# Causal mask of an attention stage: zeros written into the probabilities by GpSimd in place of mask products on TensorE, with the value products two tiles behind

## What is computed

```python
qkv = (x @ Wqkv_w + Wqkv_b).reshape(Bb, Ll, 3, Hh, dd)
scores = jnp.einsum('bhid,bhjd->bhij', q, k) * scale
causal_mask = jnp.triu(jnp.full((Ll, Ll), -10000.0, dtype=scores.dtype), 1)
attn = jax.nn.softmax(scores + causal_mask, axis=-1)
y_softmax = jnp.einsum('bhij,bhjd->bhid', attn, v)
...
    state = retention * state + Gamma * hebbian
    y_t = jnp.einsum('bhij,bhj->bhi', W_static + state, q_t)
...
y = alpha * y_softmax + (1.0 - alpha) * y_stp
```

## Time and profile before

| | |
|---|---|
| median of 3 runs | 1895.25 us (1894.73 to 1902.63) |
| the profiled execution | 1900.53 us, its span 1898.8 us |
| TensorE matmul busy | 1688.7 us (89%) |
| VectorE busy | 1551.2 us (82%) |
| ScalarE busy | 1352.6 us (71%) |
| GpSimd busy | 1223.0 us (64%) |
| granted TensorE clock, mean | 0.932 |

### The profile page before, as it was taken

One profiled execution on the slowest core, in us unless ns is written; L12 is line 12 of the kernel. 1 busy time (PEld: TensorE's weight loads), 2 busy tenths in 40 slices (PEclk: granted clock), 3 DMA queues, 4 the chain that ended last, 5 costly groups with the idle time before them and its releaser, 6 DMA issues. The chain is left out here.

```text
span 1898.8 us, 37291 instructions
## 1 busy us (share of the span) xinstructions
PE 1688.7 (89%) x13680; PEld 603.6 (32%) x13680; DVE 1551.2 (82%) x1709; ACT 1352.6 (71%) x2819; POOL 1223.0 (64%) x1146
## 2 busy tenths in 40 slices
PE   5996699999999999999999999999999999986633
PEld 3542122223333332233333322333323233323522
DVE  4457998998888899988888998989889999802967
ACT  2551288888886888888868887888678888894311
POOL 2102497768777777687777776877777788832535
PEclk9996599999998999999989999999989999997865
DMA  4674342241221421412214213122243121104402
GB/s 137 228 242 136 81 109 80 62 99 55 70 74 56 104 81 61 103 53 69 72 60 103 82 59 96 59 70 64 67 103 91 40 90 49 52 9 137 138 11 77
DMA packets 115176, 162.88 MB, mean 86 GB/s; under 512 B 29808, under 2 KB 57648, under 8 KB 114992
## 3 DMA queue, kind: packets, MB, share of 16 engines
q1 hardware_dynamic: 112608, 158.74, 28.7%
q10 hardware_dynamic: 2384, 1.77, 0.3%
HBM read 122.00 MB, written 38.01 MB: 84 GB/s over the span
## 5 line engine op out<-in xcount | busy, mean ns | idle before, releaser
L1399 DVE TENSOR_REDUCE pmax<-PS 128x2 f32<-128x1024 f32 (+2 forms) x1120 | 1213.6, 1130 | 147.0 <-PE PS L1203 117.1
L1351 ACT ACTIVATE probs<-PS 128x512 f32<-128x512 f32 (+3 forms) x2304 | 1124.6, 572 | 263.6 <-PE PS L1239 188.7
L1239 PE MATMUL PS<-Q_st,K_st 50*128 50x512 f16 (+3 forms) x1408 | 394.2, 366 | 15.8 <-DVE y_sb L1424 4.9
L1203 PE MATMUL PS<-K_st,Q_st 48*128 48x512 f16 (+3 forms) x1408 | 342.5, 362 | 13.4 <-DVE pmax L1399 11.3
L1260 PE MATMUL PS<-probs,V_g 128*17 128x512 f32 (+3 forms) x2816 | 346.1, 564 | 9.1 <-ACT o_t L1372 4.4
L1111 POOL TENSOR_TENSOR v_exp<-v_exp,k_rows 128x512 f32<-128x512 f32 x256 | 321.3, 1284 | 31.1 <-DMA v_exp<-qkv_t 30.4
L1153 POOL TENSOR_TENSOR state<-odd,q_rows 128x514 f32<-128x514 f32 x256 | 281.7, 1132 | 6.1
L1239 PE MATMUL PS<-Q_st,K_first 50*128 50x512 f16 (+3 forms) x896 | 270.5, 381 | 14.4 <-DVE shift L1414 6.9
L1203 PE MATMUL PS<-K_first,Q_st 48*128 48x512 f16 (+1 forms) x832 | 217.9, 406 | 25.3 <-DVE pmax L1399 23.7
L1260 PE MATMUL PS<-probs,V_first 128*17 128x512 f32 (+3 forms) x1792 | 232.4, 591 | 0.0
L1142 POOL COPY carry<-odd 128x4 f32<-128x4 f32 x64 | 12.0, 187 | 329.3 <-DVE odd L1434 329.3
(11 more groups left out here) (167 smaller groups left out, 1500.2 us busy)
## 6 DMA issues: line engine op xcount, KB each, us to landing
v_exp<-qkv_t SPq DMA_DIRECT2D x256, 256.0 KB
qkv_t<-proj SPq DMA_DIRECT2D x24, 512.0 KB, 3.8
qk_parts<-parts SPq DMA_DIRECT2D x16, 512.0 KB, 5.3
Q_st<-qk_parts SPq DMA_DIRECT2D x192, 32.0 KB, 3.8
v_rows<-vaug SPq DMA_DIRECT2D x8, 544.0 KB, 6.1
xin<-x SPq DMA_DIRECT2D x8, 512.0 KB, 6.2
k_rows<-qkv_t SPq DMA_DIRECT2D x16, 256.0 KB, 3.9
q_rows<-qkv_t SPq DMA_DIRECT2D x16, 256.0 KB, 6.2
```

The lines of the kernel that those rows point to most:

```text
L1203: mm = pe.matmul(PS[:, bank, 0:width], Q_st[rows, c, pair, j * P:(j + 1) * P], keys[rows, pair, blk * CH:blk * CH + width], start=True, st ...
L1239: mm = pe.matmul(PS[:, bank, 0:CH - r * P], keys[rows, pair, kt * P:(kt + 1) * P], Q_st[rows, c, pair, r * P:CH], start=True, stop=(kt < T ...
L1351: act.activation(probs[:, tile % P_SLOTS, h, 0:CH - r * P], PS[:, step[5], 0:CH - r * P], ACT.Exp, scale=SCORE_SCALE).then_inc(exp_done, 1)
L1399: dve.tensor_reduce(pmax[:, s % 2, pair * TPC + j:GH * TPC:PAIRS * TPC, blk], PS[:, bank:bank + SIDES, 0:width], AX.X, ALU.max).then_inc(m ...
```

## The change

The mask products of the score tiles go, and with them `mask_kq` and its copies; those of the maxima stay. In place of them GpSimd writes zeros: once a diagonal tile's four exponentials are done, one `affine_select` sets the future keys of the first 128 queries of all four heads to zero in `probs`, and counts `masked`. It stands in GpSimd's list at one of 15 points of a batch (0: before the wait for the scan; 1 and 2: after L1143 and L1147; 3 to 6: after each L1153; 7 and 8: after each L1121; 9: after L1128; 10: after L1132; 11 to 14: after each L1111), by a table of when each point is reached, counted in tiles. Tile 118's stands at point 13 of its batch, tile 59's and 131's at point 3; tiles 137 to 143 of a group stand in the next group's batch 0 (143 at point 9). What is left when the last group's batches end follows behind them. A diagonal tile's value products wait for `masked`. The value products of every tile are issued one tile later than before, at the end of the second tile behind; at a group's end two are left and follow each other.

```diff
--- before.py
+++ after.py
 P_SLOTS = 3
+V_LAG = 2
...
                 elif kind == "V":
-                    if pending:
+                    if len(pending) >= V_LAG:
                         values()
...
     assert not todo and max(slots) < TILES and max(moves) < TILES
-    values()
+    while pending:
+        values()
     while turns:
...
+def mask_places(period):
+    places = []
+    for tile in MASKED_TILES:
+        B, behind = divmod(tile - SLOT_AT, period)
+        later = [n for n, point in enumerate(MASK_POINTS) if point >= behind + MASK_READY]
+        places.append((B + 1, later[0], tile) if later else (B + 2, 0, tile))
+    return places
+
+
+MASKED_TILES = tuple(TILE_AT[s] + kt for s in range(NCH) for kt in range(TPC * ORDER[s], KEY_TILES[s]))
+MASK_READY = 1.1
+MASK_POINTS = (0.0, 1.35, 1.95, 2.4, 2.9, 3.3, 3.8, 4.3, 4.8, 5.3, 5.9, 6.4, 6.9, 7.4, 8.0)
...
-        mask_kq_sides = sb("mask_kq_sides", [P, SIDES, P], BF16)
...
-                        for to, of in ((ident_sides, ident_bf), (mask_qk_sides, mask_qk), (mask_kq_sides, mask_kq)):
+                        for to, of in ((ident_sides, ident_bf), (mask_qk_sides, mask_qk)):
...
-                    pool.memset(mask_kq[:, :], 0.0).then_inc(pool_setup, 1)
...
-                    pool.affine_select(out=mask_kq[:, :], in_=mask_kq[:, :], compare_op=ALU.is_ge, fill=MASKED,
-                                       base=0, pattern=[[1, P]], channel_multiplier=-1).then_inc(pool_setup, 1)
...
+                    def mask(g, tile):
+
+                        pool.wait_ge(exp_done, g * GH * TILES + GH * (tile + 1) + GH * TILES)
+                        pool.sem_inc(beats, 1)
+                        own = probs[:, tile % P_SLOTS, :, 0:P]
+                        pool.affine_select(out=own, in_=own, compare_op=ALU.is_ge, fill=0.0, base=0,
+                                           pattern=[[0, GH], [1, P]], channel_multiplier=-1).then_inc(masked, 1)
+
-                    def products(g, B):
+                    def products(g, B, masks):
...
                             pool.tensor_tensor(v_exp[:, n % RING], v_exp[:, n % RING], k_rows[:, b % 2], ALU.mult)\
                                 .then_inc(u_made, 1)
+                            masks(11 + n % BATCH)
...
                             pool.tensor_tensor(pairs[:, B % 2, k:k + 2], pairs[:, B % 2, k:k + 2],
                                                v_exp[:, slot:slot + 2, 1:CH:2], ALU.add).then_inc(pair_made, 1)
+                            masks(7 + k // 2)
...
                                            decay[:, 1, columns(B)].unsqueeze(2).broadcast_to([P, BATCH, BLOCKS]), ALU.mult)\
                             .then_inc(quad_scaled, 1)
+                        masks(9)
                         pool.wait_ge(quad_scaled, n1)
                         pool.tensor_tensor(own[:, :, 1:], own[:, :, 1:], pairs[:, B % 2, :, 1:PAIR:2], ALU.add)\
                             .then_inc(sums_made, 1)
+                        masks(10)
...
+                        masks(0)
                         pool.wait_ge(scanned, n1)
...
                             .then_inc(middle_scaled, 1)
+                        masks(1)
                         pool.wait_ge(middle_scaled, n1)
                         pool.tensor_tensor(middle, middle, pairs[:, B % 2, :, 0:PAIR:2], ALU.add).then_inc(middle_made, 1)
+                        masks(2)
...
                                                ALU.mult).then_inc(weighed, 1)
+                            masks(3 + k)
...
-                    def group_batches(g, last):
+                    def group_batches(g, last, due):
+
+                        due = list(due)
                         for B in range(N_BATCHES):
+                            def masks(point):
+                                while due and due[0][:2] <= (B, point):
+                                    mask(*due.pop(0)[2:])
...
+                        for x in due:
+                            mask(*x[2:])
...
-                    with pool.Fori(0, NG - 1) as g:
-                        group_batches(g, False)
-                    group_batches(NG - 1, True)
+                    in_group = [B < N_BATCHES for B, _, _ in mask_places(PERIOD)].count(True)
+                    group_batches(0, False, due(0, PERIOD)[:in_group])
+                    with pool.Fori(1, NG - 1) as g:
+                        group_batches(g, False, from_group_before(g) + due(g, PERIOD)[:in_group])
+                    group_batches(NG - 1, True, from_group_before(NG - 1) + due(NG - 1, LAST_PERIOD))
...
-                        mm = pe.matmul(PS[:, bank, 0:CH - r * P], keys[rows, pair, kt * P:(kt + 1) * P],
-                                       Q_st[rows, c, pair, r * P:CH], start=True, stop=(kt < TPC * c))
-                        if kt >= TPC * c:
-                            mm = add_mask(PS[:, bank, 0:P], side, mask_kq_sides)
-                        mm.then_inc(scores_ready, 1)
+                        pe.matmul(PS[:, bank, 0:CH - r * P], keys[rows, pair, kt * P:(kt + 1) * P],
+                                  Q_st[rows, c, pair, r * P:CH], start=True, stop=True).then_inc(scores_ready, 1)
...
-                        pe.wait_ge(exp_done, g * GH * TILES + GH * (tile + 1) + GH * TILES)
+                        if tile in MASKED_TILES:
+                            pe.wait_ge(masked, g * len(MASKED_TILES) + MASKED_TILES.index(tile) + 1)
+                        else:
+                            pe.wait_ge(exp_done, g * GH * TILES + GH * (tile + 1) + GH * TILES)
```

More of the change, by code:

```diff
@@ L444, in preln_attention_ffn_kernel @@
             mask_qk = sb("mask_qk", [P, P], BF16, where=pro)
-            mask_kq = sb("mask_kq", [P, P], BF16, where=pro)
             wqkv_sb = sb("wqkv_sb", [P, HALF, 3 * D], where=pro)
@@ L557, in _ @@
                         sp.wait_ge(stored[par], STORES_PER_CHUNK * (NCH // 2 + 1))
-                    sp.wait_ge(sides_made, 16 * 2 * 3 * SIDES)
+                    sp.wait_ge(sides_made, 16 * 2 * 2 * SIDES)
                 @block.gpsimd
@@ L588, in _ @@
                     pool.memset(K_first[:, :, :], SHIFT_UNIT).then_inc(shift_rows_ready, 1)
-                    pool.wait_ge(pool_setup, 13)
+                    pool.wait_ge(pool_setup, 11)
                     def power(c1):
@@ L638, in first_maxima @@
                             pe.wait_ge(k_early_loaded, 16 * STACK_LOADS)
-                            pe.wait_ge(sides_made, 16 * 2 * 3 * SIDES)
+                            pe.wait_ge(sides_made, 16 * 2 * 2 * SIDES)
                         pe.wait_ge(max_done, M_BANKS // SIDES + 1 + pairs_made - pairs_behind)
@@ L652, in first_maxima @@
                         pairs_made += 1
-                    pe.wait_ge(pool_setup, 13)
+                    pe.wait_ge(pool_setup, 11)
                     pe.wait_ge(first_weights, 16 * 2)
@@ L904, in _ @@
                                                GAIN ** -2, ALU.mult, ALU.mult))
-                    dve.wait_ge(pool_setup, 14)
+                    dve.wait_ge(pool_setup, 12)
                     link(dve.tensor_scalar(wsmall[:, 2:3], wsmall[:, 1:2], 1e-12, None, ALU.max))
@@ L1112, in products, with block_sums @@
                                 .then_inc(u_made, 1)
-                    def block_sums(g, B):
+                            masks(11 + n % BATCH)
+                    def block_sums(g, B, masks):
                         n1 = g * N_BATCHES + B + 1
@@ L1133, in block_sums, with weigh @@
                             .then_inc(sums_made, 1)
-                    def weigh(g, B):
+                        masks(10)
+                    def weigh(g, B, masks):
                         n1 = g * N_BATCHES + B + 1
@@ L1168, in group_batches, with unmasked, due, from_group_before @@
                             if not (last and B + 2 >= N_BATCHES):
-                                products(g, B + 2)
+                                products(g, B + 2, masks)
+                        for x in due:
+                            mask(*x[2:])
+                    def unmasked(point):
+                        pass
+                    def due(g, period):
+                        return [(B, point, g, tile) for B, point, tile in mask_places(period)]
+                    def from_group_before(g):
+                        return [(B - N_BATCHES, point, g - 1, tile) for B, point, tile in mask_places(PERIOD) if B >= N_BATCHES]
                     pool.sem_inc(begun, 1)
@@ L1176, in _ @@
                     lag_products_of(0, 0)
-                    products(0, 0)
+                    products(0, 0, unmasked)
                     lag_values(0, 0)
-                    block_sums(0, 0)
-                    products(0, 1)
-                    with pool.Fori(0, NG - 1) as g:
-                        group_batches(g, False)
-                    group_batches(NG - 1, True)
+                    block_sums(0, 0, unmasked)
+                    products(0, 1, unmasked)
```

(2 more changed lines are left out.)

12 lines of the change are left out of this document (6 added, 6 removed).

## The result

The changed kernel takes 1913.8 us (median, 1912.6 to 1916.1), the kernel before 1896.1 us beside it: a ratio of **1.0094** (1.0079 to 1.0108), slower, inside the range and on the side of the forecast. The profiled execution took 1916.1 us.

A forecast was written before the change was run, and what follows sets the result against it. TensorE was taken to be bound by a loop of latencies, VectorE close behind. Three groups +5.7 and the last -2.6 gave +3.1 us, with clock +10 a total of +13.1: 1908 us median, range 1878 to 1928.

The forecast's parts named there:

- The select, 0.61 us: GpSimd's 128 selects over 128x512 elements: 0.61 us each, bounds 0.29 and 1.28 us.
- 0.24 us for a diagonal tile: TensorE's diagonal tiles: the eight mask products cost 0.24 us a tile, 2.61 against a plain tile's 2.38 us.
- The two terms that I had left to the waits: Gains from removed mask products at tiles 116 and a group's end, counted with the waits there, without sizes of their own.
- Value products a tile later: at nothing: TensorE's value products in the attention stage: slots only swap widths, number and widths stay, so nothing in the sum.
- Tile 118, 2.2 us: Tiles 116 to 119: tile 118's select ends 2.2 us after its value product's slot; the stretch loses 1.8 us.
- the 0.6 us that I gave it: Tile 59: its select ends at 772.0 against a slot at 771.41, 0.6 us late, leaving 0.3 us of gain.
- A group's end, 2.8 us: Tile 143's select, in the next group's batch 0, delays its value product and the next first score: 2.8 us a group.
- The last group, -2.6 us: Last group of heads: few waits at its end, where GpSimd has nothing else to do, so a gain of 2.6 us.
- The clock, four stretches more, +10 us: TensorE's half clock: four stretches more (tile 118 in three groups, tiles 58 to 61 once), 2.5 us each, +10 us.
- in time: Rival, chance 0.22: all selects end before their value products' slots, gaining 21 us, 1874 us.
- A wash: Rival, chance 0.22: waits as summed but no more half clock, or places a little sooner; +3 us alone, 1898 us.
- Late everywhere: Rival, chance 0.14: a select of 0.9 us or more, late at tiles 15 and 35 too, clock falling at most chunks; 1930 us.

The follow-up runs named there:

- e2_nomask: Kernel before without mask products on diagonal scores, nothing in their place, value products as before: 1885.3 us, ratio 0.9932.
- e3_nomask_lag: Kernel before without mask products on diagonal scores, nothing in their place, and value products a tile later: 1880.9 us, ratio 0.9891.
- h4_last: Changed kernel with all 32 diagonal tiles of the last group masked by TensorE products again: 1906.2 us, ratio 1.0047 against the kernel before.
- e4_scratch: Changed kernel, but selects write a tile of their own and value products wait for the exponentials alone (future keys left in): 1875.4 us, ratio 0.9877.
- m1_ready: Changed kernel with every select placed half a tile earlier in GpSimd's list: 1899.3 us, ratio 1.0001 against the kernel before.
- h3_116: Changed kernel with tiles 116 to 119 of the first three groups masked by TensorE products again: 1902.3 us, ratio 1.0025 against the kernel before.
- h5_best: Changed kernel, TensorE masking tiles 59, 116 to 119, 131, 136, 140 to 143 of the first three groups and the whole last group: 1878.0 us, 0.9887.
- m2_double: Changed kernel with another select of 543 ns, into a scratch tile, ahead of each select: 1963.8 us, ratio 1.0328 against the kernel before.
- h2_end: Changed kernel with tiles 140 to 143 of the first three groups masked by TensorE products again: 1904.9 us, ratio 1.003 against the kernel before.
- e1_lag: Kernel before with value products a tile later, mask products kept: 1889.3 us, ratio 0.9955.

## Why the prediction was right, and where it only came out right

**The select, 0.61 us: right.** 636 ns in the row, near the line through 128x8 and 128x128 and far from both bounds. The 769 ns that the Trainium skill (GPSIMD Engine Reference, section 3.1) gives for a loop of 512 elements is 21% above what this row shows for the select.

**0.24 us for a diagonal tile: right** at the first tile of a chunk. What all of them give was put too low. I had 2.7 us for a group (0.9 + 0.4 + 0.3 + 0.9 + 0.2); the stretches of e2_nomask whose clock did not change have 0.9, 0.5, 0.3, 0.6, 0.6, some 0.5 and 1.0, 4.4 us. The two terms that I had left to the waits, tiles 116 and the last nine, are 1.6 of the 1.7 us of difference.

**"Value products a tile later: at nothing": wrong.** Alone it is -0.45%. The step that failed was "the cover is that the slots only swap widths": TensorE does as much work, but its stretch at half clock at tiles 128 to 134, the one of the earlier trace rows, goes with it. I had read that stretch as a price of the clock in general and had not asked whether the change moves work into it. That wider products fill the gaps of the narrow tiles there is an argument; shown is only that the lag takes the stretch away and that leaving out the mask products doesn't.

**Tile 118, 2.2 us: right in sum, one tile off.** 1.60 us falls at tile 117 and 0.81 at 118. The rows of before could have told: by the same sum tile 117's place is reached at 920.8 us and its select ends at 922.0, and the slot that its product would take is this one, 1.1 us earlier.

```profile
920.96 0.63 PE L1260 MATMUL PS<-probs,V_g 128*17 128x256 f32 x8
```

The stretch grew by 1.3 us at full clock, where I had 1.8. Tile 59 waits the 0.6 us that I gave it.

**A group's end, 2.8 us: mis-sized,** 3.6 us. The place of tile 143's select was right: 994.93 + 0.63 is 991.4 after taking off the 4.1 us by which the group began later, against my 991.1. That is 0.3 us late, and the rest is in what follows: from the product's end to the next score I had 2.6 - 0.4 = 2.2 us, for a wait of the turn that falls away, and the way is 2.50 us.

**The last group, -2.6 us: wrong,** +6.7, clock included. (The 2.0 us behind it are not its own: the rest of the kernel takes 169.6 to 173.8 us in all the kernels here, and the longest is e3_nomask_lag, which has no select.) The step that failed was that the group "is short of such waits at its end, where GpSimd has nothing else to do". Having nothing to do was part of the trouble: GpSimd is ahead of TensorE there, stops 4.41 us at the select of tile 116 in the middle of its list, and what it would have done in that time lies behind it. I had looked for selects that come late because GpSimd is behind, and not for those that come late because the one before made it wait. h4_last shows the price of the last group's selects, 9.8 us. What the stop of 4.41 us costs by itself no run takes apart: e4_scratch stops as long (4.51 us) where TensorE does not wait for the select, and its tiles 116 to 122 take 12.80 us as before (12.82), so it is the stop together with the wait behind it. m1_ready, with the same stop and a product less in the way, takes 15.03 for 16.99 us.

**The clock, four stretches more, +10 us: the amount is right by luck.** 27.3 us at half clock more are as much as four stretches of 6.8, but I had put all four into the first three groups, and there it is 6.3 us; the other 21.0 lie in the last group, where I had none. Of the places I named, the wait at tiles 117 and 118 has a stretch behind it, at tile 120, in two groups of three, and at tiles 61 and 62 there are 3.4 us more than before. Against them the stretches at tiles 132 and 133, one in each of the three groups before, are gone but for 3.4 us in the second; that is the lag's doing, which I had at nothing. And it is a balance of two larger numbers: e4_scratch, the change without its waits, has 33.6 us, 29.5 less than before, and the waits add 56.8, over eight stretches. The rule that waits between groups of matmuls put the clock back (the Trainium skill, "TensorE: Matmul & The Clock Gate", section "HAM oscillation — how this bites in real kernels") is what h3_116 shows at tiles 116 to 122: 0.85 with the stop, 1.00 without. It does not say in which group: the second has the stop too and keeps 1.00 (20.41 us).

**The sum.** I forecast gains of 11 us, waits of 14.5 and clock of 10. (TensorE's idle time at the selects, forecast near 20 us, is 23.8.) e4_scratch puts all gains, clock with them, at 1.2% or 23 us, and the waits with theirs at 2.2% or 41 us. My gains were half of what they are and my losses (24.5) six tenths, and the difference came out right. It did by luck in a second way as well. For the first three groups I had 5.7 us and 10 of clock, 15.7 in all, and they lost 5.6; for the last I had a gain of 2.6, and it lost 6.7. An error of 10 us one way stands against one of 9 the other way. What was right is the mechanism, TensorE waiting in order for selects that GpSimd's order delays, with the clock behind it; the time says little for the sizes.

Of the rivals, "in time" had the price right: e4_scratch takes 1875.4 us where nobody waits for the selects, against its 1874. But no run has all 128 selects in time. m1_ready, with the same GpSimd and another place in its list, goes part of the way (1.0001), and h5_best gets to 0.9887 with half of the masks on TensorE again. "A wash" did not hold, since the interval of the ratio begins at 1.0079. "Late everywhere" did not hold at 0.64 us, and m2_double shows that 0.54 us more are enough for it. Why the clock falls at tile 120 in the first and the third group and not in the second, whose waits are nearly the same, stays open; in h2_end, with the same selects there, it falls in the second and the third.

## What to carry to other kernels

Work that is moved to an engine with time to spare must be placed in that engine's order, not in its busy share: 128 selects on GpSimd cost nothing where nobody waited for them (e4_scratch), and 40 us where TensorE did. Check each hand-over from both sides, since an in-order engine that arrives early stops, as GpSimd did for 4.41 us, and what stands behind it in its list starts later. And when a change has two parts, time each alone: here the part costed at nothing was a gain of 0.45%, and the other gains where its selects are in time, so that both together, with 65 of the 128 diagonal tiles left to the mask products, are 1.1% faster than before.

## What the runs showed that was not expected

- Issuing the value products a tile later takes 28 of 63 us of half clock away with the same instructions (e1_lag), 2.4 to 3.1 us in each of three groups at one stretch.
- Nearly the same waits of TensorE, at tiles 116 to 122, cost 2.4 us in a group in which the clock holds and 4.8 in one in which it falls.
- GpSimd's select over 128x512 single-precision elements takes 634 to 650 ns in eight kernels, over 128x384 into half precision (bf16) 543 to 558 ns in two.
- A select placed half a tile earlier in GpSimd's list gave 0.9% (m1_ready), and one of 0.54 us ahead of it took 2.3% (m2_double).
